# A graph-attention layer on one core: the last 512 columns summed as dense blocks, the last picks and weighings in a new order

## The chip, the cores and the metric

The kernel runs on one core of a Trainium2 chip. The time is device microseconds of one execution; the number for a kernel is the median of its runs. In the profile's terms PE is TensorE, DVE is VectorE, ACT is ScalarE, POOL is GpSimd, SP is the engine that issues most DMAs, and PEld is PE's loading of weights.

## What is computed

`x` is 4096 x 128, `adj` 4096 x 4096 of zeros and ones, sparse (about two ones in a row on average, many more in the first rows and columns). Two layers, each added to `x` behind a layer norm and a ReLU:

```python
h = relu(layernorm(x))
Wh = h @ W
e = leaky_relu((Wh @ a[:128])[:, None] + (Wh @ a[128:])[None, :], 0.2)
mask = (adj > 0) | eye(4096)
x = x + softmax(where(mask, e, -9e15), axis=1) @ Wh

h = relu(layernorm(x))
sens = exp(-(1 / adj - 1) ** 2 / (2 * 0.25))
x = x + where(adj < 1.0, sens, 0.0) @ (h @ W1 + B1)
```

With entries of zero and one the second layer adds nothing (a one is not below the cutoff, and a zero gives exp of minus infinity). The kernel checks every entry for that on DVE and ACT, together with bounds on how many edges it can hold, and has a general path behind a flag for other inputs. With the inputs drawn here the general path isn't run.

## The kernel before

**Tiles and stages.** The 4096 rows are four quarters of 1024 rows. `adj` (64 MB, with its diagonal set to zero on the host) comes in 32 chunks of 2 MB: for each quarter its four blocks of 1024 columns, each in two halves of 512 rows. SP issues them in order into a ring of six slots; a slot is free when the chunk in it has been packed on PE and checked.

**From ones to edges.** PE packs eight rows of a column into one word of bits (`pack`, line 618, with a code of the column from line 614). DVE scans the words with MAX8 over segments of a bank (`scan`, 1139), each step being one block of columns. Then DVE picks the nonzero words of several steps, a piece, out of the candidates (`pick`, 1152 to 1172); PE places them across partitions (`place`, 674 and 681); DVE turns words into row numbers (`decode`, `index` at 1276). What doesn't fit a lane's own slots is shared among the lanes of a set (`pick_shared` 1188 to 1216, `place_shared` 694, `decode_shared`, `shared_index` at 1245). There are five pieces; piece 3 is the steps 12 to 14 and piece 4 is step 15 alone, which hold quarter 3.

**From edges to sums.** POOL fetches for each slot 128 rows of `node_table` (Wh and its scores, in HBM) by an indirect DMA (a gather, line 535), 66 KB each. The slots form groups of eight gathers (four in groups 5 and 9): groups 0 and 1, 3 and 4, 6, and 8 are the own slots of pieces 0, 1, 2 and 3, and groups 2, 5, 7 and 9 the shared slots of pieces 0, 1, 2 and 4. DVE weighs a group: weights from the gathered scores (1315, 1318), spread over 128 columns (1326, 1332 or 1339 by the kind of group). PE scatters the gathered rows with them into the accumulators of the quarter (`scatter`, 744). For the last group this goes by turns of one gather each (`weigh_last` 1354 and 1365, `scatter_last`).

**Beside it.** The first 128 columns, which are dense, are transposed and weighed as a whole (1409, `add_columns` 729). A node's own weight goes by a diagonal (ACT 962, `add_own` 736). A quarter ends with `epilogue` (1420, 1425) and the store of its rows; the last quarter with `finish_last` and `finish` (1435, 1439). `check` is one pass of DVE over a chunk (1111) or two of ACT (929, 938).

**What sets the order.** Each engine's program is written out by hand. It loops over chunks i, and tables say in which iteration a step stands: on DVE `SCAN_AT`, `PICK_AT`, `DECODE_AT`, `EPILOGUE_AT`, `WEIGH_AT`, and `CHECK_LATE` for checks that are put off; on PE `PLACE_AT`, `PLACE_BEHIND`, `SCATTER_AT`, `ADD_COLUMNS_AT`, `ADD_OWN_AT`; on ACT `OWN_WEIGHTS_AT`. What stands behind the loop is written in order. POOL's gathers are in the order of the groups, each waiting for its index and for a free place among the gathered rows. Engines run in order, so an instruction that waits holds all behind it.

## Time and profile before

| | |
|---|---|
| median of 3 runs | 215.99 us (215.91 to 216.35) |
| the profiled execution | 216.57 us, span 214.8 us |
| PE, DVE, ACT, POOL busy | 72%, 83%, 88%, 60% of the span |
| mean granted clock of PE | 0.923 |
| chunk DMAs | 32 of 2 MB; 76.83 MB moved in all, 358 GB/s over the span |

Until about 190 us the DMA engines are busy all the time with the chunks, and the other engines keep up with them at various distances. The last chunk lands at about 191.8 us; what follows is the rest of quarter 3: picking, gathering, weighing, summing and storing. No engine is busy all through that stretch. The busy shares of the whole span therefore say little on it, and the views to read are the chain of waits of the last 75 us and the engines' instructions in order of time in it. Times in these views count from the span's start.

### The profile page before, as it was taken

What the parts mean: (1) busy time and instruction counts of PE and PEld (TensorE: products, weight loads), DVE (VectorE), ACT (ScalarE), POOL (GpSimd) and SP (SyncE); (2) the same over time, 40 slices, a digit from 0 to 9 for tenths busy, and PEclk for the clock granted to TensorE, in tenths of its full rate; (3) what the DMA queues carried; (4) which work ended last, traced back from release to release, by engine and by line L of the source; (5) the groups of instructions that cost most, each with busy time, mean ns of one, the idle gap of its engine ahead of it and who ended that gap; (6) DMA issues with size and microseconds to landing.
All of it is one profiled execution on the core that took longest, in us unless ns stands there. A gap on an engine that the chain in (4) does not pass through costs nothing.

```text
span 214.8 us, 3127 instructions
## 1 busy us (share of the span) xinstructions
PE 155.6 (72%) x914; PEld 102.5 (48%) x928; DVE 177.4 (83%) x529; ACT 189.5 (88%) x207; POOL 129.7 (60%) x140
## 2 busy tenths in 40 slices
PE   0188779994849665599749978599393967799572
PEld 0076565441425342387535635286231654667561
DVE  7993999999997999989474695995796599859855
ACT  0699988499999999999999999799999994999960
POOL 3980002196001788889777888889077788868350
PEclk9999999998888999889976999889878899999887
DMA  5999999999999999999999999999999999972313
GB/s 158 347 415 410 412 406 413 404 410 405 414 421 408 404 392 400 402 393 396 398 388 387 392 403 389 399 389 395 400 408 390 390 397 393 407 283 45 117 23 104
DMA packets 22403, 76.83 MB, mean 358 GB/s; under 512 B 2671, under 2 KB 3270, under 8 KB 22384
## 3 DMA queue, kind: packets, MB, share of 16 engines
q1 hardware_dynamic: 18912, 71.31, 84.9%
q0 software_dynamic: 2912, 5.22, 7.2%
q8 instruction: 8, 0.13, 0.3%
q10 hardware_dynamic: 560, 0.08, 0.2%
q14 instruction: 11, 0.09, 0.1%
HBM read 74.08 MB, written 4.23 MB: 365 GB/s over the span
## 4 chain that ended last, share of the span: by engine, by line
DMA 27%; DVE 27%; PE 19%; issue 11%; POOL 9%; ACT 5%; POOLq 0%; DVEq 0%; ACTq 0%; SPq 0%
DMA adj_ring<-adj_apart 23%; POOL gathered_rows L535 9%; DVE summed L1111 8%; PE bank L618 7%; DMA gathered_rows<-node_table,shared_index 4%; ACT spread L898 3%; PE bank L744 3%; PE bank L653 2%; DVE hub_w L1382 2%; PE bank L729 2%; DVE x_sb L1425 2%; PE bank L736 2%; DVE shared_slots L1197 1%; DVE cand L1139 1%; DVE stats L1091 1%
## 5 line engine op out<-in xcount | busy, mean ns | idle before, releaser
L535 POOL DMA_INDIRECT gathered_rows<-node_table,index x48 | 69.3, 1444 | 38.6 <-DVE index L1276 24.5
L929 ACT ACTIVATE trash_a<-adj_ring,below_one 128x4096 fp8e4<-128x4096 f32 x19 | 70.4, 3704 | 5.3 <-DMA adj_ring<-adj_apart 4.7
L618 PE MATMUL bank<-adj_ring,pack_w 128*128 128x512 bf16 x242 | 70.7, 423 | 4.5 <-DMA adj_ring<-adj_apart 3.4
L938 ACT ACTIVATE trash_a<-adj_ring 128x4096 fp8e4<-128x4096 f32 x19 | 68.7, 3614 | 0.5
L1111 DVE SCALAR_TENSOR_TENSOR summed<-adj_ring 128x4096 fp8e4<-128x4096 f32 x13 | 58.2, 4480 | 7.5 <-DMA adj_ring<-adj_apart 7.4
L535 POOL DMA_INDIRECT gathered_rows<-node_table,shared_index x24 | 36.8, 1535 | 9.8 <-issue 7.0
L618 PEld LDWEIGHTS bank<-adj_ring,pack_w 128*128 128x128 bf16 x248 | 25.0, 103 | 35.5 <-issue 9.8
L1139 DVE MAX8 cand<-bank 128x8 f32<-128x120 f32 (+25 forms) x82 | 23.3, 351 | 2.8 <-PE bank L618 2.8
L744 PE MATMUL bank<-gathered_rows,spread 128*128 128x129 f32 x160 | 21.0, 283 | 3.0 <-DVE spread L1365 1.8
L744 PEld LDWEIGHTS bank<-gathered_rows,spread 128*128 128x128 f32 x160 | 19.5, 196 | 4.8 <-issue 4.4
L614 PE MATMUL bank<-codes,code_w 128*128 128x512 bf16 x24 | 10.6, 443 | 8.7 <-DMA adj_ring<-adj_apart 8.7
L653 PE MATMUL bank<-whe,hub_w 128*128 128x129 f32 x64 | 10.2, 316 | 5.7 <-DVE hub_w L1386 5.7
L898 ACT ACTIVATE spread<-x_sb,shift,rstd 128x128 f32<-128x128 f32 x32 | 13.3, 501 | 0.3 <-DVE shift L1103 0.3
L653 PEld LDWEIGHTS bank<-whe,hub_w 128*128 128x128 f32 x64 | 9.4, 225 | 7.2 <-DVE hub_w L1386 6.9
L482 POOL PARTITION_ALL_REDUCE ends_all<-ends x1 | 1.4, 1440 | 17.4 <-DVE ends L1507 17.4
L556 PE MATMUL bank<-ident,spread 128*128 128x128 f32 x32 | 6.5, 337 | 7.2 <-ACT spread L898 7.2
L568 PE MATMUL bank<-w_sb,gathered_rows 128*128 128x130 f32 x64 | 10.6, 318 | 1.2 <-ACT whe L912 0.9
L568 PEld LDWEIGHTS bank<-w_sb,gathered_rows 128*128 128x128 f32 x64 | 9.5, 227 | 2.4 <-ACT gathered_rows L904 1.8
L614 PEld LDWEIGHTS bank<-codes,code_w 128*128 128x128 bf16 x32 | 3.8, 119 | 13.7 <-DMA adj_ring<-adj_apart 10.4
L1409 DVE SCALAR_TENSOR_TENSOR col_w<-r_rows,hub_whe,bank 128x512 f32<-128x512 f32 (+1 forms) x6 | 4.2, 701 | 7.1 <-PE bank L598 7.1
L962 ACT ACTIVATE own_w<-ident,w_self 128x128 f32<-128x128 f32 x32 | 9.7, 386 | 0.2 <-PE bank L736 0.2
L1382 DVE TENSOR_SCALAR hub_w<-r_hub,whe 128x128 f32<-128x128 f32 x32 | 8.9, 352 | 0.0
(188 smaller groups left out, 237.0 us busy)
## 6 DMA issues: line engine op xcount, KB each, us to landing
adj_ring<-adj_apart SPq DMA_DIRECT2D x32, 2048.0 KB, 23.3
node_table<-gathered_rows POOLq DMA_DIRECT2D x4, 520.0 KB, 9.3
x_sb<-in_x SPq DMA_DIRECT2D x8, 256.0 KB, 5.8
out<-x_sb SPq DMA_DIRECT2D x3, 512.0 KB, 14.4
gathered_rows<-node_table,index POOLq DMA_INDIRECT x48, 5.6
gathered_rows<-node_table,shared_index POOLq DMA_INDIRECT x24, 5.7
out<-x_sb SPq DMA_DIRECT2D x2, 192.0 KB, 2.0
out<-x_sb SPq DMA_DIRECT2D x1, 128.0 KB, 2.0
```

What stands on the lines that cost most here:

```text
L535: pool.indirect_dma_start(out=rows[:, g % RING_GROUPS * GE + t, :], out_offset=None, in_=table, in_offset=bass.IndirectOffsetOnAxis(ap=row ...
L568: last = nc.tensor.matmul(bank[6 + half][:, b * (D + 2):(b + 1) * (D + 2)], hT[:, nb * P:(nb + 1) * P], w0_sb[:, :], start=(b == 0), stop= ...
L614: nc.tensor.matmul(to[:, :], code_w[:, 2 * c + half, :], codes[:, :], start=True, stop=False, skip_group_check=True)
L618: last = nc.tensor.matmul(to[:, :], pack_w[:, k, :], ring_hi[:, i % AR, at:at + BW], start=False, stop=(k == KB - 1), skip_group_check=True)
L653: last = nc.tensor.matmul(bank[7][:, 0:E1], hub_w[:, m % 2, b, :], whe[:, 4 * HUB_ORDER[m] + b, ONE:ONE + E1], start=(m + b == 0), stop=(m ...
L744: return nc.tensor.matmul(acc_of(SUPER_OF_GROUP[g], t), spread[:, g % 2, at * KB:(at + 1) * KB, :], rows[:, g % RING_GROUPS * GE + turn, G ...
L898: last = nc.scalar.activation(hn_block(b), x_sb[:, b, :], ACT.Identity, bias=shift[:, b:b + 1], scale=rstd[:, b:b + 1])
L929: nc.scalar.activation(trash_a[:, :], ring[:, i % AR, :], ACT.Sign, bias=below_one[:, :], scale=-1.0, accum_out=signs[:, n:n + 1], saturat ...
L938: nc.scalar.activation(trash_a[:, :], ring[:, i % AR, :], ACT.Abs, accum_out=sizes[:, n:n + 1], saturate=False).then_inc(checked_a, 1)
L1111: nc.vector.scalar_tensor_tensor(trash_v, ring[:, i % AR, :], 1.0, ring[:, i % AR, :], ALU.is_ge, ALU.not_equal, accum_out=bad_v[:, n:n + ...
L1139: last = nc.vector.max(cand[:, at * 8:(at + 1) * 8], word_bank(step, half)[:, lo:hi])
L1382: last = nc.vector.tensor_scalar(hub_w[:, m % 2, b, :], r_hub[:, :], whe[:, nb, QA:QA + 1], whe[:, nb, AA:AA + 1], ALU.mult, ALU.max)
```

## The change

For quarter 3 the chunks are cut in another way. Chunk 28 is 512 columns (2048 to 2559) of all 1024 rows; chunks 29 and 30 are columns 1024 to 2047 in two halves; chunk 31 is the last 512 columns (2560 to 3071), laid out by the host with columns on partitions: four blocks of 128 columns x 1024 rows, each with a DMA and a semaphore of its own. Chunk 31 is neither packed nor scanned. DVE makes a block's weights in one instruction (`weigh_dense`), and PE adds the block with eight matmuls (`add_dense`). The rows of `node_table` for these 512 columns (`dense_whe`) come by one DMA on SP ahead of chunk 20 and lie in `summed`; checks from chunk 14 on therefore write their unused result to `hub_mask`, and the dense weights lie in the ring slot of chunk 26.

Piece 2's shared slots go to sets of eight lanes instead of four, so that group 7 has four gathers instead of eight. Two tables of factors (`r_oct2`, halves of `r_quad`) change with it.

The order: pick(3) in iteration 29 rather than 30, and PE's place(3) directly behind pack(29); weigh(7), which stood behind the loop, in iteration 28; check(26) in iteration 26 behind weigh(5), rather than 27; epilogue(1) at 27 and epilogue(2) at 30; scatters, column sums and own sums accordingly; ACT's own weights of quarter 3 at 29.

```diff
+NARROW, DENSE = 28, CHUNKS - 1
 def chunk(i):
+    if i >= NARROW:
+        return SG - 1, 1 if i in (29, 30) else 2, int(i > 29)
...
-PIECES = [..., ((8, 9, 10, 11), 24, 8, 32, 4),
+PIECES = [..., ((8, 9, 10, 11), 24, 8, 32, 8),
...
-CHECK_LATE = {22: 22, 27: 26, 29: 28}
-SCAN_AT = {2 * n + 2: n for n in range(STEPS - 1)}
-PICK_AT = {8: 0, 16: 1, 24: 2, 30: 3}
-DECODE_AT = {9: 0, 17: 1, 25: 2, 31: 3}
+CHECK_LATE = {22: 22, 26: 26, 28: 28}
+SCAN_AT = {**{2 * n + 2: n for n in range(STEPS - 2)}, 29: 14}
+PICK_AT = {8: 0, 16: 1, 24: 2, 29: 3}
+DECODE_AT = {9: 0, 17: 1, 25: 2, 30: 3}
...
-WEIGH_AT = {13: 0, 17: 1, 18: 2, 21: 3, 25: 4, 26: 5, 28: 6}
-SCATTER_AT = {14: 0, 17: 1, 19: 2, 22: 3, 26: 4, 27: 5, 30: 6}
-PLACE_AT = {8: 0}
-PLACE_BEHIND = {15: 1, 23: 2, 29: 3}
+WEIGH_AT = {13: 0, 17: 1, 18: 2, 21: 3, 25: 4, 26: 5, 27: 6, 28: 7}
+SCATTER_AT = {14: 0, 17: 1, 19: 2, 22: 3, 25: 4, 26: 5, 28: 6, 29: 7}
+PLACE_AT = {8: 0, 29: 3}
+PLACE_BEHIND = {15: 1, 23: 2}
...
-ADD_COLUMNS_AT = {13: 0, 21: 1, 28: 2}
-EPILOGUE_AT = {20: 0, 28: 1}
-OWN_WEIGHTS_AT = {8: 0, 17: 1, 22: 2, CHUNKS: 3}
-ADD_OWN_AT = {13: 0, 21: 1, 29: 2}
+ADD_COLUMNS_AT = {13: 0, 21: 1, 27: 2}
+EPILOGUE_AT = {20: 0, 27: 1, 30: 2}
+OWN_WEIGHTS_AT = {8: 0, 17: 1, 22: 2, 29: 3}
+ADD_OWN_AT = {13: 0, 21: 1, 27: 2}
...
+                if i == DENSE:
+                    for b in range(DB):
+                        sp.dma_start(dense_adj[:, b, :], adj_tail[1, b]).then_inc(dense_ready[b], 16)
+                    return
...
+                if i == 20:
+                    sp.wait_ge(table_stored, 16 * SG)
+                    sp.wait_ge(checked_v, DVE_CHECKED.index(14))
+                    sp.dma_start(dense_whe, table[DENSE_AT:DENSE_AT + BW, :].rearrange("(p b) c -> p b c", b=DB)).then_inc(
+                        dense_whe_loaded, 16)
...
+            def add_dense(b):
+                pe.wait_ge(dense_set, b + 1)
+                pe.wait_ge(dense_whe_loaded, 16)
+                for t in range(KB):
+                    nc.tensor.matmul(acc_of(SG - 1, t), dense_w[:, b, t, :], dense_whe[:, b, GQ:GQ + E1], start=False,
+                                     stop=True, skip_group_check=True)
...
-            scatter(7)
+            add_columns(SG - 1, range(6))
+            add_own(SG - 1, range(6))
             place(4)
-            add_columns(SG - 1)
+            add_columns(SG - 1, range(6, KB))
+            add_own(SG - 1, range(6, KB))
+            add_dense(0)
             place_shared(4)
-            add_own(SG - 1)
+            add_dense(1)
+            add_dense(2)
             scatter(8)
+            add_dense(3)
             scatter_last(0)
...
+            def weigh_dense(b):
+                dve.wait_ge(dense_ready[b], 16)
+                if b == 0:
+                    dve.wait_ge(dense_whe_loaded, 16)
+                    dve.wait_ge(packed, 27)
+                    dve.wait_ge(col_turned, 2 * (SG - 1) + 1)
+                    dve.wait_ge(checked_v, DVE_CHECKED.index(26) + 1)
+                nc.vector.scalar_tensor_tensor(dense_w[:, b, :, :].rearrange("p t m -> p (t m)"),
+                                               r_rows[:, :, :].rearrange("p t m -> p (t m)"), dense_whe[:, b, AQ:AQ + 1],
+                                               dense_adj[:, b, :], ALU.max, ALU.mult).then_inc(dense_set, 1)
...
-            weigh(7)
             scan(STEPS - 1)
             pick(4)
-            epilogue(2)
+            weigh_dense(0)
             pick_shared(4)
+            weigh_dense(1)
             decode_shared(4)
+            weigh_dense(2)
             weigh(8)
+            weigh_dense(3)
             weigh_last(0)
```

What the tables do to the engines' order stands out at three places. The first is DVE behind weigh(5), whose last row is the spread at 1339 (now 1439). In the kernel before, with 1409 the column products (`col_w`) of chunks 26 and 27, 1111 the check of chunk 26 and 1139 scan(13):

```order
L1339 TENSOR_TENSOR spread<-same,hq_of_e 128x512 x2
L1409 SCALAR_TENSOR_TENSOR col_w<-r_rows,hub_whe,bank 128x8x64
L1111 SCALAR_TENSOR_TENSOR summed,bad<-adj_ring 128x4096
L1409 SCALAR_TENSOR_TENSOR col_w<-r_rows,hub_whe,bank 128x8x64
L1139 MAX cand<-bank 128x8 x5
```

And now, where 1180 is the check and 1509 the first column product:

```order
L1406 TENSOR_TENSOR same<-r_pair,gathered_rows 128x128
L1409 TENSOR_TENSOR same<-same,shared_on 128x128
L1439 TENSOR_TENSOR spread<-same,hq_of_e 128x512 x2
L1180 SCALAR_TENSOR_TENSOR hub_mask,bad<-adj_ring 128x4096
L1509 SCALAR_TENSOR_TENSOR col_w<-r_rows,hub_whe,bank 128x8x64
```

The check of chunk 26 has gone ahead of the first column product. The second place is DVE from there to the check of chunk 28. In the kernel before (1139 scan(13), then weigh(6) to 1326, epilogue(1) to 1425, the check, scan(14) and the start of pick(3)):

```order
L1139 MAX cand<-bank 128x8 x5
L1315 TENSOR_TENSOR edge_w<-r_slots,gathered_rows 128x64
L1318 TENSOR_TENSOR edge_w<-edge_w,bits_i 128x64
L1326 TENSOR_TENSOR spread<-edge_w,lane_of_p 128x1024
L1420 RECIPROCAL rden<-bank 128x3 x2
L1420 RECIPROCAL rden<-bank 128x2
L1425 SCALAR_TENSOR_TENSOR x_sb<-bank,rden,x_sb 128x128 x8
L1111 SCALAR_TENSOR_TENSOR summed,bad<-adj_ring 128x4096
L1139 MAX cand<-bank 128x8 x5
L1152 TENSOR_REDUCE fullest<-cand 128x1
```

And now (1520 and 1525 epilogue(1), 1406 to 1417 weigh(6), 1509 the second column product, 1208 scan(13), 1406 with `r_oct` to 1430 weigh(7), 1180 the check):

```order
L1520 RECIPROCAL rden<-bank 128x3 x2
L1520 RECIPROCAL rden<-bank 128x2
L1525 SCALAR_TENSOR_TENSOR x_sb<-bank,rden,x_sb 128x128 x8
L1406 TENSOR_TENSOR edge_w<-r_slots,gathered_rows 128x64
L1409 TENSOR_TENSOR edge_w<-edge_w,bits_i 128x64
L1417 TENSOR_TENSOR spread<-edge_w,lane_of_p 128x1024
L1509 SCALAR_TENSOR_TENSOR col_w<-r_rows,hub_whe,bank 128x8x64
L1208 MAX cand<-bank 128x8 x5
L1406 TENSOR_TENSOR same<-r_oct,gathered_rows 128x256
L1409 TENSOR_TENSOR same<-same,shared_on 128x256
L1430 TENSOR_TENSOR spread<-same,quad_of_e 128x512 x2
L1180 SCALAR_TENSOR_TENSOR hub_mask,bad<-adj_ring 128x4096
```

epilogue(1) has gone ahead of weigh(6), and weigh(7), which stood behind pick_shared(3), ahead of the check of chunk 28. The third place is PE's tail. In the kernel before, from the packing of chunk 30 on (618; 744 is a scatter, 674 place(4), 729 the columns, 694 place_shared(4), 736 the own sums):

```order
L618 MATMUL bank<-adj_ring,pack_w 128x512 x4
L744 MATMUL bank<-gathered_rows,spread 128x129 x8
L618 MATMUL bank<-adj_ring,pack_w 128x512 x8
L744 MATMUL bank<-gathered_rows,spread 128x129 x8
L674 MATMUL bank<-slots,own_oct 16x8 x8
L729 MATMUL bank<-hub_whe,col_w 128x129 x8
L694 MATMUL bank<-turn_of_tq,stats 128x4
L736 MATMUL bank<-whe,own_w 128x129 x8
L744 MATMUL bank<-gathered_rows,spread 128x129 x16
```

And now, from scatter(7) on (806 is a scatter, 676 the packing of chunk 30, 789 the columns, 797 the own sums, 732 place(4), 772 the dense blocks, 752 place_shared(4)):

```order
L806 MATMUL bank<-gathered_rows,spread 128x129 x8
L676 MATMUL bank<-adj_ring,pack_w 128x512 x8
L789 MATMUL bank<-hub_whe,col_w 128x129 x6
L797 MATMUL bank<-whe,own_w 128x129 x6
L732 MATMUL bank<-slots,own_oct 16x8 x8
L789 MATMUL bank<-hub_whe,col_w 128x129 x2
L797 MATMUL bank<-whe,own_w 128x129 x2
L772 MATMUL bank<-summed,adj_ring 128x129 x8
L752 MATMUL bank<-turn_of_tq,stats 128x4
L772 MATMUL bank<-summed,adj_ring 128x129 x16
L806 MATMUL bank<-gathered_rows,spread 128x129 x8
L772 MATMUL bank<-summed,adj_ring 128x129 x8
```

scatter(7) has moved from behind the last packing to ahead of it, where it follows place(3); one block of eight dense matmuls stands ahead of place_shared(4), two behind it, and one between scatter(8) and the last scatters.

## Rows read from the trace of the kernel before

**Rows 1.** Chain of waits, 140 to 215: start us, length us, what it was

```profile
180.07 5.01 POOL gathered_rows L535
...
185.38 6.33 DMA gathered_rows<-node_table,shared_index
...
211.78 0.61 DVE x_sb L1439 x2
```

**Rows 2.** POOL in time: start us, us, line, operation [idle before, what ended it]

```profile
169.26 0.99 POOL L535 DMA_INDIRECT gathered_rows<-node_table,shared_index  x1 [0.30 <-issue]
170.56 4.33 POOL L535 DMA_INDIRECT gathered_rows<-node_table,shared_index  x1 [0.30 <-issue]
...
188.89 1.08 POOL L535 DMA_INDIRECT gathered_rows<-node_table,index  x1 [1.42 <-DVE index L1276]
...
192.90 1.91 POOL L535 DMA_INDIRECT gathered_rows<-node_table,index  x1 [0.30 <-issue]
...
204.12 1.21 POOL L535 DMA_INDIRECT gathered_rows<-node_table,shared_index  x1 [0.30 <-issue]
...
206.94 1.00 POOL L535 DMA_INDIRECT gathered_rows<-node_table,shared_index  x1 [0.30 <-issue]
```

**Rows 3.** DVE in time, 163 to 213, columns as before

```profile
163.44 1.34 DVE L1339 TENSOR_TENSOR spread<-same,hq_of_e 128x512 f32<-128x512 f32 x2
...
169.60 4.42 DVE L1111 SCALAR_TENSOR_TENSOR summed<-adj_ring 128x4096 fp8e4<-128x4096 f32 x1
...
179.79 4.42 DVE L1111 SCALAR_TENSOR_TENSOR summed<-adj_ring 128x4096 fp8e4<-128x4096 f32 x1
...
184.13 1.49 DVE L1139 MAX8 cand<-bank 128x8 f32<-128x24 f32 x5
...
187.95 0.17 DVE L1276 SCALAR_TENSOR_TENSOR index<-words_i,empty_i 128x8 int32<-128x8 int32 x1
...
191.79 0.43 DVE L1315 TENSOR_TENSOR same<-r_quad,gathered_rows 128x256 f32<-128x256 f32 x1 [2.13 <-DMA gathered_rows<-node_table,shared_index]
...
192.72 1.23 DVE L1332 TENSOR_TENSOR spread<-same,quad_of_e 128x1024 f32<-128x1024 f32 x1
193.87 1.43 DVE L1139 MAX8 cand<-bank 128x8 f32<-128x272 f32 x4
...
196.37 2.16 DVE L1425 SCALAR_TENSOR_TENSOR x_sb<-bank,rden,x_sb 128x128 f32<-128x128 f32 x8
...
201.87 0.16 DVE L1245 TENSOR_TENSOR shared_index<-shared_column,shared_empty 128x4 int32<-128x4 int32 x1
...
202.73 0.22 DVE L1315 TENSOR_TENSOR edge_w<-r_slots,gathered_rows 128x64 f32<-128x64 f32 x1
...
203.24 1.22 DVE L1326 TENSOR_TENSOR spread<-edge_w,lane_of_p 128x1024 f32<-128x1024 f32 x1
...
208.88 0.17 DVE L1435 RECIPROCAL rden<-bank 128x3 f32<-128x3 f32 x1
```

**Rows 4.** DMA issues, 160 to 190: bytes each, median us to landing

```profile
gathered_rows<-node_table,shared_index POOLq DMA_INDIRECT x8, 5.9
```

**Rows 5.** DMA issues, 188 to 210

```profile
gathered_rows<-node_table,index POOLq DMA_INDIRECT x8, 3.2
```

**Rows 6.** PE in time, 160 to 213, columns as in rows 2

```profile
164.55 0.39 PE L614 MATMUL bank<-codes,code_w 128*128 128x512 bf16 x1 [3.46 <-DMA adj_ring<-adj_apart]
164.77 1.87 PE L618 MATMUL bank<-adj_ring,pack_w 128*128 128x512 bf16 x4
...
176.42 1.06 PE L618 MATMUL bank<-adj_ring,pack_w 128*128 128x512 bf16 x4
...
194.09 2.02 PE L744 MATMUL bank<-gathered_rows,spread 128*128 128x129 f32 x16 [0.26 <-DVE spread L1332]
```

**Rows 7.** ACT in time, 175 to 213, columns as in rows 2

```profile
181.44 3.71 ACT L929 ACTIVATE trash_a<-adj_ring,below_one 128x4096 fp8e4<-128x4096 f32 x1 [2.83 <-DMA adj_ring<-adj_apart]
```

**Rows 8.** Stretch: engines' busy us (count), then PEclk, DMA share, GB/s

```profile
164.50:168.50 4.00, 3.95 (x12) 1.46 (x13) 0.28 (x1) 3.97 (x3) 3.09 (x4) 0.57 1.03 389
```

More of the change, by code:

```diff
@@ L61, in chunk, with banks_of, step_of, packed_by @@
     return s, (first + i % (2 * CC) // 2) % CC, i % 2
+def banks_of(step):
+    c = chunk(2 * step)[1]
+    return [2 * c] if 2 * step == NARROW else [2 * c, 2 * c + 1]
+def step_of(i):
+    return STEPS - 1 if i in (29, 30) else i // 2
+def packed_by(step):
+    return 2 * step + 2 if step < STEPS - 2 else 2 * step + 1
+def scanned_by(step):
+    return sum(len(banks_of(m)) for m in range(step + 1))
 def column_step(s):
     return next(n for n in range(CC * s, CC * s + CC) if chunk(2 * n)[1] == 0)
-PIECES = [((0, 1, 2, 3), 32, 16, 32, 4), ((4, 5, 6, 7), 24, 16, 16, 4), ((8, 9, 10, 11), 24, 8, 32, 4),
+PIECES = [((0, 1, 2, 3), 32, 16, 32, 4), ((4, 5, 6, 7), 24, 16, 16, 4), ((8, 9, 10, 11), 24, 8, 32, 8),
           ((12, 13, 14), 16, 8, 0, 8), ((15,), 8, 0, 32, 8)]
@@ L101, in piece_segments @@
     s = SUPER_OF_PIECE[n]
-    columns = {chunk(2 * step)[1] for step in PIECES[n][0]}
-    return [x for x in SEGMENTS[s] if x[0] // 2 in columns]
+    banks = {b for step in PIECES[n][0] for b in banks_of(step)}
+    return [x for x in SEGMENTS[s] if x[0] in banks]
 NCAND = max(len(piece_segments(n)) for n in range(len(PIECES))) * 8
@@ L292, in gnn_program @@
         oct_words = placed[0:LANES, 1, :]
[L293 removed]
+        s_by_oct = [general_mem[:, NB * 32 + n * KB * KB * OL:NB * 32 + (n + 1) * KB * KB * OL] for n in range(2)]
         verdict = cand[:, 0:NBAD]
@@ L792, in _ @@
             lane_scores()
-            for i in range(CHUNKS):
+            for i in range(DENSE):
                 pack(i)
```

190 lines of the change are left out of this document (120 added, 70 removed).

## The prediction

> **What bounds the kernel now.** I read the chain of waits first, for the last 75 us, then the orders in time of the engines that it names. Up to 160 us the chain is mostly the stream of adjacency chunks; from there to the end it is POOL and DVE by turns. Two of POOL's gathers, which take 1.00 us elsewhere, stand there with 5.01 and 4.33 us; then comes the landing of the rows that the last of group 7's gathers fetched, 6.33 us from 185.38 [rows 1, 2]. weigh(7) waits 2.13 us for those rows [rows 3]. The chain goes on over scan(15), epilogue(2), pick_shared(4) and the last four gathers, and ends with the output tiles of quarter 3.
>
> The long gathers have one cause that the trace repeats. Gather 170.56 starts under check(26) (169.60 + 4.42 = 174.02) and ends at 174.89; gather 180.07 starts under check(28) (to 184.21) and ends at 185.08; gather 192.90 starts under the spread of weigh(7) (to 193.95) and ends at 194.81 [rows 1 to 3]. So a gather that begins while DVE runs an instruction with two operands in SBUF ends 0.87 us after that instruction. Undisturbed, gathers follow one another every 1.30 us [rows 2].
>
> **Part 1, the last 512 columns are summed densely.** Removed: packing and scanning of these columns, before a half of chunks 30 and 31. Added on DVE: four products of 128x1024. None is in the trace; a quarter of a check (4.42 for 4096 elements) is 1.10, and the spread of 128x1024 takes 1.23 [rows 3]. I take 1.2: 4.8 us in four pieces. Added on PE: four times eight matmuls of the 128x129 form; eight (16 passes in the trace) take 2.02 [rows 6], so 8.1 us, of which three blocks lie in PE's waits before group 8 is weighed. The fourth does not: it stands between scatter(8) and the last scatters, +2.0. The dense rows' table (0.27 MB more on SP) is as much as the four gathers of 66 KB that group 7 loses, so the chunks should keep their times. ACT's own_weights(3) goes into the 2.83 us for which ACT waits for chunk 29 [rows 7]: no gain and no loss, because ACT is not in the chain there.
>
> **Part 2, check(26) goes behind weigh(5).** weigh(5) ends at 163.44 + 1.34 = 164.78, and chunk 26 is there at 164.55 [rows 3, 6]. The check starts between 164.9 and 165.9; I take 165.4, so it ends at 169.8. It now catches another gather: the eighth of group 6, at 169.26 - 2 x 1.30 = 166.66, ends at 170.7 (0.87 behind) rather than 167.7. Group 7 has four gathers instead of eight; they start at 171.0, 172.3, 173.6 and 174.9. Under this load a gather lands 5.9 us after its start [rows 4], so the group's rows are there at 180.8; with 0.3 either way I take 180.5. Before, they were there at 191.7.
>
> **Part 3, weigh(7) goes ahead of check(28) and of the third pick.** DVE gets to it at about 179: group 6's held gather lands 4.9 behind its end, at 175.6; weigh(6) 1.7 like weigh(8), scan(13) at most scan(14)'s 1.49, and the column product, half of a dense one, 0.6 [rows 3]. Then it waits for group 7 until 180.5, in place of the 2.13 us before. Behind that waiting instruction on DVE stand check(28), scan(14) and pick(3), and for these wait place(3) on PE, and then POOL, which has nothing to fetch until index(3). weigh(7) took 2.16 (191.79 to 193.95); with its spread in two halves 2.3: to 182.8. check(28) takes 4.34 up to scan(14) (179.79 to 184.13): 187.1. scan(14) has two segments instead of five, 1.49 x 2/5 = 0.6, I take 0.7: 187.8. From the end of the scan (185.62) to index(3) it is 2.33 [rows 3]: index(3) at **190.1, against 187.95**. That is +2.15, the step on which the forecast rests most. epilogue(2) is no longer between pick(4) and pick_shared(4), but ahead of scan(15), which is worth 2.4 to DVE's tail; the products take more than that back.
>
> **Part 4, twelve gathers in a row.** The first gather starts 0.94 after index(3) [rows 2, 3]: 191.04. Eight of group 8 and four of the last group follow: 191.04 + 12 x 1.30 - 0.30 = 206.3 if nothing holds them. Before, the last ended at 206.94 + 1.00 = 207.94 [rows 2]. But the dense products and the spread of weigh(8) now lie over just these gathers. Each can hold one back by 0 to 1.0 us (spread 192.72 cost 0.91, spread 203.24 cost 0.21) [rows 2, 3], five of them by 0 to 5; I take 0.55 each, the mean of the two, of which 1.9 falls on group 8 in front of its eighth gather (three products and a part of a fourth instruction). That gather ends at 191.04 + 8 x 1.30 - 0.30 + 1.9 = 203.0, so counts from 202.0; it lands 3.2 later [rows 5], at 205.2. weigh(8) takes 1.73 (202.73 to 204.46) [rows 3]: 206.9. Before: 204.46, so +2.4.
>
> DVE itself is ready by then: epilogue(2) ends near 194.3 (2.4 of work behind scatter(7), which PE reaches after place(3)), scan(15) takes 1.43, with pick(4) 2.0, so with the first product 197.5; pick_shared(4) and the index took 3.34 behind epilogue(2) (198.53 to 201.87), with the second product in between 202.0; the third 203.7 [rows 3]. So group 8's rows are what comes last, by 1.5.
>
> **The end.** PE: scatter(8) 206.9 to 208.8, the fourth dense block to 210.7, two short scatters to 211.5. From the start of finish_last(0), which follows them, to the last output tile it was 208.88 to 212.39 [rows 1, 3], 3.5: to 215.0, **+2.6**.
>
> **PE's clock.** Where PE had waited 3.46 us for chunk 26, four packing matmuls behind took 1.87 against 1.06 elsewhere, and the granted clock of that stretch was 0.57, near the lower of the two levels (1.2 of 2.4 GHz) [rows 6, 8]. In the new order PE has nothing between pack(29), done near 184.6, and place(3) near 188.7, a wait of 4 us, so scatter(7) and pack(30) can run at half: 0 to +1.5 on epilogue(2) and scan(15), most of it hidden behind the gathers. I take +0.4.
>
> Sum: +3.0. The profiled execution took 216.57 us with a span of 214.8; it would be 219.6, and the median of the runs is 0.58 lower: **219.0**.
>
> **A rule of the skill against it.** The trace shows gathers held by DVE, but not the reverse: check(26) at 169.60 began under gather 169.26 (to 170.25) and took 4.42, the same as check(28) at 179.79, under which none was running when it began [rows 1 to 3]. The Trainium skill (SBUF — State Buffer, "SBUF: two separate sides") says of the port pair that the two engines share that whichever starts first gets it for the whole instruction and the other is fully blocked. By that rule a product would wait for the gather under it as well, which is rival D. The row speaks against it, for this form of instruction.
>
> **The rivals.**
> A. As forecast, +3.0.
> B. About as before. The products slip past the gathers' starts (0.6 instead of 1.9 on group 8), PE stays at its upper level (-0.4) and group 7's rows land at 179.5 (-1.0): -2.7, so 216.3. For it: spread 203.24 cost only 0.21.
> C. Faster. These products, and check(26) where it now stands, do not hold gathers as the three instructions of the trace did. Group 7's rows are then there before DVE is (179), so index(3) comes 1.5 sooner; group 8 loses its 1.9, the clock's 0.4 goes, and the last two PE blocks run 0.3 closer: 219.0 - 4.1 = 214.9. It decides in favour of the change when the sum of holds on groups 6 to 8 is under about 1 us. Against it: all three long gathers follow the same rule to 0.02 us.
> D. Worse. The products wait for gathers as well as holding them: five by half of a gather's 1.00 is +2.5, 221.5.
> E. The change doesn't do what it says: a word with more edges than its slots now hold sends the kernel down its general path, many times the time. Counted from the reference's inputs, the fullest words fit; 0.01.
>
> **How the numbers follow.** A 0.58, B 0.20, C 0.16, D 0.05, E 0.01. A spreads from 217 to 221.5 with the holds (0 to 5) and the landing (179 to 181.5). The range leaves out half of C and half of D, and E: 215.0 to 221.5. A measurement of this kernel tells 0.2% (0.43 us) from no change, so "same" is 215.56 to 216.42. Of C 0.13 is faster and 0.03 the same; of B 0.03 faster, 0.07 the same, 0.10 slower; A, D and E are slower. Together: faster 0.16, same 0.10, slower 0.74.
>
> **What would show it.** Right: DVE waits at weigh(7) until 180 to 181; index(3) at 189.5 to 190.7, its first gather 0.94 later; the eighth gather of group 6 with 3 to 4.4 us; twelve gathers without a wait for an index between them, some of 1.3 to 2.0; weigh(8) ending at 206 to 208. Wrong: no wait at weigh(7), or index(3) before 188.5; a wait of POOL for shared_index (then the products on DVE, not the gathers, set the end); a granted clock of 1 behind place(3) takes the 0.4 off; and if DVE is still at weigh_last when the last dense block ends, the 2.0 for that block is wrong.

## The result and the profile after

| | before | changed |
|---|---|---|
| median | 216.17 us (215.91 to 216.86, 4 runs) | 220.38 us (220.02 to 220.50, 4 runs) |
| profiled execution, span | 216.57, 214.8 | 220.36, 218.6 |
| ratio of the runs | | 1.0177 (95%: 1.0148 to 1.0205) |
| index(3) starts at | 187.95 | 190.95 |
| from there to the last output tile | 24.44 | 25.33 |
| last output tile done | 212.39 | 216.28 |

By the ratio of the runs the change costs 1.5 to 2.0%, about 3.8 us; the two medians lie 4.2 us apart. The profiled executions differ by 3.89 us in the end of the last output tile: 3.00 of it is there when index(3) starts, 0.89 comes behind it.

The page of the changed kernel: the span, the busy times, the granted clock in 40 slices, and two lines on the chain that ended last.

```profile
span 218.6 us, 3283 instructions
PE 161.4 (74%) x993; PEld 108.3 (50%) x993; DVE 182.0 (83%) x533; ACT 190.1 (87%) x209; POOL 121.1 (55%) x136
PEclk9999999997967998899958999999579999769999
## 4 chain that ended last, share of the span: by engine, by line
DMA 32%; DVE 28%; PE 23%; issue 9%; ACT 5%; SPq 2%; DVEq 0%; ACTq 0%
```

POOL, which had 9% of the chain before, is out of it, and PE has gone from 19% to 23%. The four gathers saved show in POOL's busy time (129.7 to 121.1 us). The granted clock has a dip to 7 and 6 tenths in slices 35 and 36 (186 to 197 us), where it had its full value before (1.00 from 182 to 202). The kernel before has a dip of its own, 0.57 from 202 to 206.

DVE in order of time in the changed kernel, to compare with [rows 3] (lines moved: 1180 is a check, 1350 index(3), 1369 a dense product, 1319 shared_index, 1406 and 1439 belong to the weighings, 1454 to weigh_last, 1520 is epilogue(2), 1535 finish_last):

```profile
164.93 1.34 DVE L1439 TENSOR_TENSOR spread<-same,hq_of_e 128x512 f32<-128x512 f32 x2
166.19 4.41 DVE L1180 SCALAR_TENSOR_TENSOR hub_mask<-adj_ring 128x4096 fp8e4<-128x4096 f32 x1
...
175.92 0.23 DVE L1406 TENSOR_TENSOR edge_w<-r_slots,gathered_rows 128x64 f32<-128x64 f32 x1 [2.37 <-issue]
...
181.23 0.42 DVE L1406 TENSOR_TENSOR same<-r_oct,gathered_rows 128x256 f32<-128x256 f32 x1 [1.65 <-issue]
...
183.36 4.42 DVE L1180 SCALAR_TENSOR_TENSOR hub_mask<-adj_ring 128x4096 fp8e4<-128x4096 f32 x1
...
190.95 0.17 DVE L1350 SCALAR_TENSOR_TENSOR index<-words_i,empty_i 128x8 int32<-128x8 int32 x1
...
194.32 0.30 DVE L1520 RECIPROCAL rden<-bank 128x3 f32<-128x3 f32 x3 [1.66 <-PE bank L806]
...
198.63 1.28 DVE L1369 SCALAR_TENSOR_TENSOR adj_ring<-r_rows,summed,adj_ring 128x1024 f32<-128x1024 f32 x1
...
202.39 1.26 DVE L1369 SCALAR_TENSOR_TENSOR adj_ring<-r_rows,summed,adj_ring 128x1024 f32<-128x1024 f32 x1
...
203.96 0.16 DVE L1319 TENSOR_TENSOR shared_index<-shared_column,shared_empty 128x4 int32<-128x4 int32 x1
...
204.82 1.33 DVE L1369 SCALAR_TENSOR_TENSOR adj_ring<-r_rows,summed,adj_ring 128x1024 f32<-128x1024 f32 x1
206.07 0.21 DVE L1406 TENSOR_TENSOR edge_w<-r_slots,gathered_rows 128x64 f32<-128x64 f32 x1
...
211.40 0.28 DVE L1454 SCALAR_TENSOR_TENSOR same<-r_oct,gathered_rows,shared_on 128x64 f32<-128x64 f32 x1 [0.91 <-DMA gathered_rows<-node_table,shared_index]
...
212.76 0.18 DVE L1535 RECIPROCAL rden<-bank 128x3 f32<-128x3 f32 x1 [0.55 <-PE bank L806]
```

Up to index(3) this is what the prediction's parts 2 and 3 describe, about a microsecond later: the check of chunk 26 stands right behind weigh(5), DVE waits 1.65 us in front of weigh(7), and check(28), scan(14) and pick(3) follow. Behind index(3) it is not: DVE waits 1.66 us for scatter(7) in front of epilogue(2), and from there to weigh(8) at 206.07 it works almost without a gap. POOL in the same stretch, against [rows 2]:

```profile
166.85 4.63 POOL L579 DMA_INDIRECT gathered_rows<-node_table,index  x1 [0.30 <-issue]
...
175.69 1.00 POOL L579 DMA_INDIRECT gathered_rows<-node_table,shared_index  x1 [0.30 <-issue]
...
191.90 1.08 POOL L579 DMA_INDIRECT gathered_rows<-node_table,index  x1 [11.16 <-DVE index L1350]
...
198.52 1.00 POOL L579 DMA_INDIRECT gathered_rows<-node_table,index  x1 [0.30 <-issue]
...
201.13 1.00 POOL L579 DMA_INDIRECT gathered_rows<-node_table,index  x1 [0.30 <-issue]
204.89 1.00 POOL L579 DMA_INDIRECT gathered_rows<-node_table,shared_index  x1 [2.77 <-DVE shared_index L1319]
...
207.49 1.18 POOL L579 DMA_INDIRECT gathered_rows<-node_table,shared_index  x1 [0.30 <-issue]
```

The eighth gather of group 6 is held as forecast (4.63 us, 0.88 behind the check's end at 170.60), and group 7's last gather lands 5.5 us after 175.69. But group 8's eight gathers run through unheld: the first dense product starts 0.11 us after the sixth gather (198.63 and 198.52) and ends 0.08 us into the seventh, and the second comes when all eight are done. POOL then waits 2.77 us for shared_index, as it did before the change (2.79 us), so the twelve are not in a row. PE in order of time, and three stretches of it (columns as in rows 8):

```profile
189.54 0.57 PE L732 MATMUL bank<-slots,own_oct 128*16 128x8 f32 x16 [4.36 <-issue]
...
190.49 3.79 PE L806 MATMUL bank<-gathered_rows,spread 128*128 128x129 f32 x16
194.07 2.37 PE L676 MATMUL bank<-adj_ring,pack_w 128*128 128x512 bf16 x8
...
209.88 1.95 PE L772 MATMUL bank<-summed,adj_ring 128*128 128x129 f32 x16
```

```profile
185.20:189.50 4.30, 0.00 (x0) 0.00 (x0) 4.16 (x10) 4.27 (x4) 0.00 (x0) 0.83 1.02 412
189.50:194.00 4.50, 4.46 (x34) 4.47 (x35) 2.16 (x13) 4.47 (x4) 1.80 (x2) 0.50 0.58 231
194.00:198.00 4.00, 4.00 (x26) 2.69 (x25) 3.68 (x16) 3.97 (x4) 3.08 (x4) 0.89 0.19 47
```

PE does nothing for 4.36 us ahead of place(3), and scatter(7) then runs at 0.50 of the full clock, the lower of the two levels (1.2 of 2.4 GHz): 3.79 us against 2.02 in [rows 6]. That is the wait in front of epilogue(2).

### The profile page after: what moved, and what is told of

It reads as the page before. It is cut to its first block, busy times and chain, and to the rows that moved or that the text cites. A ratio compares the mean times of both kernels' runs of the same rounds, so it can differ in the third digit from the quotient of the medians.

```text
span 218.6 us, 3283 instructions
## 1 busy us (share of the span) xinstructions
PE 161.4 (74%) x993; PEld 108.3 (50%) x993; DVE 182.0 (83%) x533; ACT 190.1 (87%) x209; POOL 121.1 (55%) x136
## 4 chain that ended last, share of the span: by engine, by line
DMA 32%; DVE 28%; PE 23%; issue 9%; ACT 5%; SPq 2%; DVEq 0%; ACTq 0%
DMA adj_ring<-adj_apart 32%; DVE summed L1180 8%; PE bank L676 8%; PE bank L806 5%; ACT spread L963 3%; DVE hub_w L1482 3%; DVE cand L1208 3%; PE bank L772 2%; PE bank L672 2%; PE bank L789 2%; DVE x_sb L1525 2%; PE bank L797 2%; SPq L438 2%; DVE adj_ring L1369 1%; DVE stats L1158 1%
## 5 line engine op out<-in xcount | busy, mean ns | idle before, releaser
L579 POOL DMA_INDIRECT gathered_rows<-node_table,index x48 | 73.2, 1525 | 47.9 <-DVE index L1350 34.2
L676 PE MATMUL bank<-adj_ring,pack_w 128*128 128x512 bf16 x232 | 66.5, 420 | 4.6 <-DMA adj_ring<-adj_apart 4.6
L676 PEld LDWEIGHTS bank<-adj_ring,pack_w 128*128 128x128 bf16 x232 | 23.6, 104 | 35.9 <-issue 9.9
L1180 DVE SCALAR_TENSOR_TENSOR hub_mask<-adj_ring 128x4096 fp8e4<-128x4096 f32 x6 | 26.5, 4417 | 6.9 <-DMA adj_ring<-adj_apart 6.9
L1180 DVE SCALAR_TENSOR_TENSOR summed<-adj_ring 128x4096 fp8e4<-128x4096 f32 x7 | 31.4, 4492 | 0.1
L579 POOL DMA_INDIRECT gathered_rows<-node_table,shared_index x20 | 23.9, 1193 | 8.6 <-issue 5.5
L806 PEld LDWEIGHTS bank<-gathered_rows,spread 128*128 128x128 f32 x160 | 20.6, 206 | 3.0 <-issue 2.5
L672 PE MATMUL bank<-codes,code_w 128*128 128x512 bf16 x30 | 13.5, 451 | 5.4 <-DMA adj_ring<-adj_apart 5.4
L711 PEld LDWEIGHTS bank<-whe,hub_w 128*128 128x128 f32 x64 | 8.2, 200 | 8.8 <-DVE hub_w L1486 8.6
L772 PE MATMUL bank<-summed,adj_ring 128*128 128x129 f32 x64 | 8.0, 278 | 1.3 <-DVE adj_ring L1369 1.3
```

Source lines behind the costliest of these rows:

```text
L579: pool.indirect_dma_start(out=rows[:, g % RING_GROUPS * GE + t, :], out_offset=None, in_=table, in_offset=bass.IndirectOffsetOnAxis(ap=row ...
L672: nc.tensor.matmul(to[:, :], code_w[:, 2 * c + half, :], codes[:, :], start=True, stop=False, skip_group_check=True)
L676: last = nc.tensor.matmul(to[:, :], pack_w[:, k, :], ring_hi[:, i % AR, at:at + BW], start=False, stop=(k == KB - 1), skip_group_check=True)
L711: last = nc.tensor.matmul(bank[7][:, 0:E1], hub_w[:, m % 2, b, :], whe[:, 4 * HUB_ORDER[m] + b, ONE:ONE + E1], start=(m + b == 0), stop=(m ...
L806: return nc.tensor.matmul(acc_of(SUPER_OF_GROUP[g], t), spread[:, g % 2, at * KB:(at + 1) * KB, :], rows[:, g % RING_GROUPS * GE + turn, G ...
L1180: nc.vector.scalar_tensor_tensor(trash_v[int(i >= 14)], ring[:, i % AR, :], 1.0, ring[:, i % AR, :], ALU.is_ge, ALU.not_equal, accum_out=b ...
```

## Experiments

Four things could stand behind the 3.9 us: the load of the dense rows' table, weigh(7) ahead of the third pick, PE's clock, and the dense work itself. Here is what each kernel gave; the ratio is to the kernel before on the same chip, and the last three columns, in us, are from the profiled execution.

| kernel | ratio (95%) | index(3) | from there to the last tile | last tile |
|---|---|---|---|---|
| before | 1 | 187.95 | 24.44 | 212.39 |
| changed | 1.0177 (1.0148 to 1.0205) | 190.95 | 25.33 | 216.28 |
| e1 table loaded late | 1.0170 (1.0132 to 1.0208) | 190.07 | 25.33 | 215.40 |
| e2 weigh(7) behind the pick | 1.0141 (1.0110 to 1.0173) | 187.07 | 29.82 | 216.89 |
| e3 PE kept busy | 1.0134 (1.0094 to 1.0174) | 190.78 | 24.96 | 215.74 |
| e4 nothing dense | 1.0093 (1.0057 to 1.0129) | 191.34 | 23.56 | 214.90 |
| e5 e2 with PE kept busy | 1.0119 (1.0068 to 1.0169) | 186.62 | 28.34 | 214.96 |
| e6 nothing dense, PE kept busy | 1.0045 (1.0020 to 1.0069) | 189.43 | 23.77 | 213.20 |
| e7 e1, e5, epilogue(2) later | 0.9987 (0.9957 to 1.0017) | 186.53 | 26.30 | 212.83 |
| e8 e7, shared index first | 1.0188 (1.0153 to 1.0224) | 186.11 | 30.92 | 217.03 |
| e9 e7, two steps reordered | 0.9958 (0.9935 to 0.9981) | 186.02 | 25.42 | 211.44 |
| e10 eight lanes alone | 1.0008 (0.9979 to 1.0038) | 188.49 | 24.43 | 212.92 |

The profiled execution is one of the timed ones. It lies between 0.4 us under and 1.4 us over its kernel's median, and index(3) shifts with the stream of chunks: e4 changes nothing ahead of index(3) and has it 0.4 us later than the changed kernel, e6 has the same work there as e3 and has it 1.35 us earlier. A difference of less than a microsecond in these columns therefore proves little by itself.

**e1: the table's load.**

```diff
-                if i == 20:
+                if i == DENSE:
                     sp.wait_ge(table_stored, 16 * SG)
```

> The load of the dense rows' table goes from ahead of chunk 20 to ahead of chunk 31. Theory: that load sets the chunk stream back (chunk 26 landed at 166.08 against 164.50), and check(26), the held eighth gather, group 7's rows, weigh(7), check(28) and index(3) hang on chunk 26; chunks 20 to 30 land 0.9 to 1.2 us earlier and the time falls by as much, to 219.2 to 219.5. Rival: the stream is late for another reason or has slack here; the time stays within 0.4 us of the changed kernel's 220.38.

The first packing of chunk 20 in the kernel before, the changed one and e1:

```profile
131.40 0.39 PE L614 MATMUL bank<-codes,code_w 128*128 128x512 bf16 x1 [0.41 <-DMA adj_ring<-adj_apart]
```

```profile
132.36 0.39 PE L672 MATMUL bank<-codes,code_w 128*128 128x512 bf16 x1 [0.89 <-DMA adj_ring<-adj_apart]
```

```profile
131.71 0.39 PE L672 MATMUL bank<-codes,code_w 128*128 128x512 bf16 x1 [0.41 <-DMA adj_ring<-adj_apart]
```

The stream of chunks as a whole lies up to a microsecond earlier or later from one execution to the next, so one pair of times says little here. The gap between two landings says more: in the six profiled executions with the load ahead of chunk 20 (changed, e2 to e6) that chunk landed 6.25 to 6.48 us behind chunk 19, in five without it (before, e1, e7, e8, e10; e9's landing is not in its trace) 5.56 to 5.58. So the load costs the stream 0.7 to 0.9 us at this place, and most of it stays: from the landing of chunk 16 to that of chunk 30 it is 79.5 to 80.1 us in the six and 79.0 to 79.4 in the five. In e1 index(3) and the last tile are both 0.88 us earlier. The timed runs put e1 at 219.76 us, 0.6 below the changed kernel but within the intervals of both ratios: the mechanism is shown at chunk 20, its worth in the whole time is not told from zero.

**e2: weigh(7) behind the pick.**

```diff
-WEIGH_AT = {..., 27: 6, 28: 7}
-SCATTER_AT = {..., 28: 6, 29: 7}
+WEIGH_AT = {..., 27: 6}
+SCATTER_AT = {..., 28: 6, 30: 7}
...
                     pick_shared(DECODE_AT[i])
+                    if DECODE_AT[i] == HANDED:
+                        weigh(7)
```

> weigh(7) goes behind the third pick's pick_shared(3), where it was before, and scatter(7) behind the packing of chunk 30; all else as changed. Theory (weigh(7)'s wait of 1.65 and its 2.13 us of work stand in front of index(3)): index(3) at 187.2 instead of 190.95, PE's wait ahead of place(3) shrinks from 4.36 to about 1 us and its granted clock stays at the upper level; weigh(7) then ends at 191.0, scatter(7) at 193.0, epilogue(2) starts at 193.0 instead of 194.32: 1.3 us less, 219.1. Rival (index(3) hangs on the chunks or on the pack of chunk 28, not on weigh(7)): index(3) after 189.5, and the time 220.4 to 222.5, since weigh(7)'s 2.1 us now stand behind it.

DVE (first two lines) and PE in e2:

```profile
187.07 0.17 DVE L1350 SCALAR_TENSOR_TENSOR index<-words_i,empty_i 128x8 int32<-128x8 int32 x1
...
194.92 0.30 DVE L1520 RECIPROCAL rden<-bank 128x3 f32<-128x3 f32 x3 [3.96 <-PE bank L806]
```

```profile
187.76 2.76 PE L676 MATMUL bank<-adj_ring,pack_w 128*128 128x512 bf16 x8 [0.99 <-DMA adj_ring<-adj_apart]
191.11 3.78 PE L806 MATMUL bank<-gathered_rows,spread 128*128 128x129 f32 x16 [0.59 <-DVE spread L1430]
```

index(3) is where the theory put it, 3.9 us sooner. But in the profiled execution PE, with waits of 0.6 to 1.2 us, falls to 0.57 of its clock from 187.7 on all the same, scatter(7) takes 3.78 us, and DVE waits 3.96 us for it; the last tile comes no sooner. This execution, with 221.08 us, is the slowest of e2's five. The other four took 219.23 to 219.74, some 0.6 to 1.2 us under the changed kernel's median and not far from the theory's 219.1. Three of them have a mean granted clock of 0.94 over the span against 0.91 in the profiled one; whether the clock stayed up behind index(3) in these, no trace shows. The ratio is not apart from the changed kernel's by the intervals. So the theory's step on the path is right, its step on the clock failed in the execution that can be read, and what weigh(7)'s place is worth by itself stays open.

**e3: PE kept busy.**

```diff
+                if i == 29:
+                    pe.wait_ge(scanned, scanned_by(12))
+                    for k in range(18):
+                        nc.tensor.matmul(bank[1][:, :], pack_w[:, k % KB, :], codes[:, :], start=True, stop=True,
+                                         skip_group_check=True)
                 if i in PLACE_AT:
```

> 18 matmuls into an unused bank are put on PE between the packing of chunk 29 and place(3), with no other change; their result is not used. Theory: PE's clock fell to its lower level behind the 4.36 us in which it had nothing to do, and scatter(7) with 3.79 us kept DVE waiting 1.66 us in front of epilogue(2); with the clock kept up scatter(7) takes 2.0, the wait is 0 to 0.2 and the end comes 1.5 to 1.7 us earlier, 218.8. Rival (as predicted, most of the slow clock is hidden behind the gathers): 0.4 or less, 220.0 or more.

PE, DVE and POOL in e3 (1374 is a dense product, 1411 weigh(8)):

```profile
190.32 2.03 PE L806 MATMUL bank<-gathered_rows,spread 128*128 128x129 f32 x16
```

```profile
196.75 1.28 DVE L1374 SCALAR_TENSOR_TENSOR adj_ring<-r_rows,summed,adj_ring 128x1024 f32<-128x1024 f32 x1
...
200.50 1.26 DVE L1374 SCALAR_TENSOR_TENSOR adj_ring<-r_rows,summed,adj_ring 128x1024 f32<-128x1024 f32 x1
...
205.53 0.28 DVE L1411 TENSOR_TENSOR edge_w<-r_slots,gathered_rows 128x64 f32<-128x64 f32 x1 [1.26 <-issue]
```

```profile
197.03 1.87 POOL L579 DMA_INDIRECT gathered_rows<-node_table,index  x1 [0.30 <-issue]
...
200.50 2.14 POOL L579 DMA_INDIRECT gathered_rows<-node_table,index  x1 [0.31 <-issue]
```

scatter(7) is back at 2.03, epilogue(2) starts at 192.42 without a wait, 1.9 us sooner. Only 0.54 of this reaches the last tile (0.96 in the medians, 219.42 against 220.38). The dense products, now earlier, lie over the gathers of group 8 and hold two of them (1.87 and 2.14 us, ending 0.87 and 0.88 behind the product), and weigh(8) waits 1.26 us. The profile names nothing that ended this wait, but the last of group 8's gathers landed at 205.45, just ahead of it. This is the mechanism of the prediction's part 4. The clock alone does not decide whether it comes: with the clock kept up as well, e5 has no gather of group 8 held, and e7 and e9 have one each.

**e4 and e6: nothing dense**, without and with e3's matmuls. Every `weigh_dense` and `add_dense` is taken out, so these kernels leave out 512 columns of quarter 3.

> The four dense products on DVE and the four dense blocks on PE are left out, so the last quarter's sums lack 512 columns; loads, checks and all else stay. Theory (DVE's own work sets the tail): weigh(8) starts 3.6 us earlier at 202.4, the last four gathers from 202.5, the end about as in the kernel before, 4.0 to 4.4 us earlier, 216.2. Rival (as predicted, group 8's gathers set weigh(8), and only the last PE block is on the path): no gather had been held by a product, so 2.0 us earlier, 218.4.

> As e4 (dense products and blocks left out, so 512 columns lack in the last quarter's sums), with e3's 18 unused matmuls ahead of place(3). Theory (three limits close together: DVE's dense work, PE's clock, the held gathers; in e4 the slow clock took the first one's place): weigh(8) at about 201.0 to 202.0, the last gather ends at about 207.0, the end 3.4 us before e4's and 4.8 before the changed kernel's, 215.6. Rival (the dense work is worth the 2 us of e4 and the clock 0.6 to 0.9 by itself): 217.5 to 218.0.

The rivals' numbers hold in both, 218.42 and 217.70 us, and the theories fall: without the dense work the tail is far from 4 us shorter. The reason that e4's rival gave does not hold: group 8's rows are there at 204.01, and DVE comes to weigh(8) at 205.04 without a wait. In e4 DVE is rid of the 3.6 us of the products and then waits for PE, which packs chunk 30 at half clock (2.88 us), and for place(4) and place_shared(4) (1.12 and 0.60 us). In e6 PE has nothing to do from 199 to 204 once the dense blocks are gone, and pays at the very end: the granted clock is 0.50 from 204 to 210, and DVE waits 2.43 us for PE ahead of finish_last(0). So the clock is not out of the picture there as the theory had it. PE in e6 in that stretch:

```profile
198.66 0.38 PE L752 MATMUL bank<-turn_of_tq,stats 16*128 16x4 f32 x2 [1.59 <-DVE stats L1286]
204.15 6.21 PE L806 MATMUL bank<-gathered_rows,spread 128*128 128x129 f32 x28 [5.11 <-DVE spread L1418]
```

From index(3) to the last tile the dense work is worth 1.2 us with PE kept busy (24.96 in e3, 23.77 in e6) and 1.8 without (25.33, 23.56), of the 4.8 us that DVE spends on it. The ratios make it 1.8 to 1.9 us in both pairs.

**e5: e2 with PE kept busy.**

```diff
+                if i == 29:
+                    keep_up(5)
                 pack(i)
+                if i == 30:
+                    keep_up(6)
...
                     place(PLACE_AT[i])
+                if i == 29:
+                    keep_up(8)
```

Here `keep_up(n)` issues n of e3's matmuls, and e2's edit is in it too.

> As e2 (weigh(7) behind pick_shared(3), scatter(7) behind the packing of chunk 30), and PE kept busy by 19 unused matmuls into a free bank: 5 ahead of pack(29), 8 behind place(3), 6 behind pack(30). Theory (in e2 the 3.7 us earlier index(3) was lost to PE's lower clock, scatter(7) 3.78 us and DVE's wait of 3.96): packing and scatter(7) at 2.0 us each, epilogue(2) starts at 193.1 against 194.92 in e2 and 194.32 in the changed kernel, and the time is 1.2 us under the changed kernel's, 219.2. Rival (weigh(7) behind the pick costs on DVE what it gives on POOL, whatever the clock): 220.0 or more.

epilogue(2) starts at 192.98 and the time is 219.27, as the theory said; the last tile comes at 214.96, 1.32 before the changed kernel's. Of 4.3 us that index(3) gains, 3.0 are given back behind it, since weigh(7) and the wait for scatter(7) (2.47 us) now stand there on DVE. The ratio is not apart from e2's or the changed kernel's by the intervals, so what the unused matmuls bring in e5 is not shown by the timed runs.

**e7: e1 and e5 together, and epilogue(2) behind pick(4).** The last edit:

```diff
-EPILOGUE_AT = {20: 0, 27: 1, 30: 2}
+EPILOGUE_AT = {20: 0, 27: 1}
...
             pick(4)
+            epilogue(2)
             weigh_dense(0)
```

> e1 and e5 together (table load ahead of chunk 31, weigh(7) behind pick_shared(3), PE kept busy), and epilogue(2) behind pick(4), where it was before the change. Theory (the causes found add up: stream 0.9, weigh(7) ahead of index(3) 3.7, clock 1.9, less what DVE's own work takes back): index(3) at 186.2, weigh(7) ends at 190.1, weigh(8) at 203.7, the end 4.0 to 4.4 us before the changed kernel's, 216.0 to 216.4, level with the kernel before. Rival (the dense products hold gathers as soon as these run under them, up to 1 us each): 217 to 218.

216.39 us, level with the kernel before. DVE's two remaining waits in e7:

```profile
192.89 0.31 DVE L1532 RECIPROCAL rden<-bank 128x3 f32<-128x3 f32 x3 [0.51 <-PE bank L806]
...
209.31 0.18 DVE L1547 RECIPROCAL rden<-bank 128x3 f32<-128x3 f32 x1 [1.55 <-PE bank L806]
```

scan(15) and pick(4) now fill the time in which scatter(7) runs. From e5 to e7 the ratio falls by more than the intervals, and from index(3) to the last tile the profiled execution gains 2.04 us. The late table leaves that stretch as it was in e1 (25.33), so this gain is epilogue(2)'s place. So the 3.8 us that the changed kernel loses can be won back without touching the dense layout, by the order of the steps, the place of the table's load and the 19 unused matmuls together. The same without the matmuls was not run, so it is not shown that the order alone would do.

**e8: the shared index ahead of the products.**

```diff
-            weigh_dense(0)
             pick_shared(4)
-            weigh_dense(1)
             decode_shared(4)
+            weigh_dense(0)
+            weigh_dense(1)
             weigh_dense(2)
```

On PE place_shared(4) goes ahead of `add_dense(0)`.

> As e7, with the first three dense products behind decode_shared(4) instead of around it, and place_shared(4) ahead of the dense blocks on PE. Theory (in e7 DVE and PE set the end, the last four gathers come in time): shared_index of piece 4 at 198 instead of 200.1, weigh(8) as in e7, the end the same to 0.4 us earlier, 215.6 to 216.2. Rival (the last gathers set the end in e7): 2.0 us earlier, 214.2.

220.74 us, worse than either said. PE in e8, and a stretch of it:

```profile
198.26 0.38 PE L752 MATMUL bank<-turn_of_tq,stats 16*128 16x4 f32 x2 [1.57 <-DVE stats L1297]
201.32 7.68 PE L772 MATMUL bank<-summed,adj_ring 128*128 128x129 f32 x48 [2.68 <-DVE adj_ring L1381]
```

```profile
198.00:202.00 4.00, 1.05 (x5) 0.97 (x6) 3.56 (x13) 3.97 (x4) 1.68 (x2) 0.60 0.09 20
```

With the products bunched behind the index, PE waits 1.57 and 2.68 us, its clock falls to 0.60 and then 0.55, and three dense blocks take 7.68 us instead of 6.0. scatter(8) starts at 208.84, against 204.64 in e7. Of these 4.2 us 1.7 is the slower clock; the rest is that all three blocks now begin at 201.32, where in e7 the first had run at 196.95. The blocks had also been PE's filling. Neither theory had the clock or this queue on PE in it.

**e9: two steps of e7 reordered.**

```diff
-            epilogue(2)
             weigh_dense(0)
+            epilogue(2)
...
-            finish_last(0)
             weigh_last(3)
+            finish_last(0)
```

> As e7, with the first dense product ahead of epilogue(2) instead of behind it, and weigh_last(3) ahead of finish_last(0). Theory (in e7 DVE works without a gap from 188 to 205 but for 0.51 us in which it waits for scatter(7), and then waits 1.55 us for PE while weigh_last(3) stands behind that wait): the product fills the first wait, -0.5, and weigh_last(3) with 0.8 us the second, -0.8; the end 1.3 us before e7's, 215.1, below the kernel before by 0.6 to 0.8%. Rival (the product holds a gather of group 8, or the last gather lands after the wait): as e7, level with the kernel before.

215.47 us against 216.31 for the kernel before in the same runs: 0.9958 (0.9935 to 0.9981), 1.39 us before e7 in the last tile, 0.88 of it behind index(3). That is less than the theory's 0.6 to 0.8%, but clear of no change: e9 is faster than the changed kernel, and by 0.2 to 0.65% faster than the kernel before. From e7 the intervals do not part it. DVE in e9:

```profile
191.85 1.28 DVE L1381 SCALAR_TENSOR_TENSOR adj_ring<-r_rows,summed,adj_ring 128x1024 f32<-128x1024 f32 x1
193.06 0.30 DVE L1532 RECIPROCAL rden<-bank 128x3 f32<-128x3 f32 x3
```

Both waits are gone. The product did hold a gather of group 8 (1.62 us), as the rival had it, but weigh(8) did not wait for it.

**e10: eight lanes alone.** The kernel before with piece 2's sets of eight lanes, hence four gathers in group 7; the order and the chunks are those of before.

> The kernel before with one part of the change alone: piece 2's shared slots in sets of eight lanes, so that group 7 has four gathers instead of eight; chunks, order and tail as before, nothing dense. Theory (in the kernel before the 2.13 us wait for group 7's rows lay beside another: scan(15) needs the packing of chunk 31, which landed at 191.80 and was packed at 193.83): the wait at weigh(7) is gone, scan(15) still starts at 193.6 to 194.0, and the time is within 0.4 us of the kernel before. Rival (that wait was the path, as the chain of waits has it): 2.1 us less than the kernel before.

DVE in e10 (1371 with `r_oct` is weigh(7), 1173 scan(15)):

```profile
190.16 0.43 DVE L1371 TENSOR_TENSOR same<-r_oct,gathered_rows 128x256 f32<-128x256 f32 x1
...
194.21 1.43 DVE L1173 MAX8 cand<-bank 128x8 f32<-128x272 f32 x4 [1.83 <-PE bank L647]
```

1.0008 (0.9979 to 1.0038): no gain, to within some 0.5 us. The wait for gathered rows that the chain of waits names in the kernel before [rows 1, 3] goes, and a wait of 1.83 us for the packing of chunk 31 comes up one step behind it. It had been there all the time, underneath.

## Why the prediction was right, point by point

- **Direction and size.** +3.0 was forecast, to 219.0; the ratio of the runs gives +3.8, and the median is 220.4, inside the range. Up to index(3) the change came by the mechanism forecast. That the part behind index(3) fits as well, +0.85 forecast (3.0 - 2.15) and +0.89 in the trace, is luck: another wait sets it, as part 4 and the clock below show.
- **The first reading of the chain: too strong.** "Mostly the stream" up to 160 us isn't what the page shows: chunk loads are 23% of the whole chain, about 50 of these 160 us. Nothing in the forecast rests on this.
- **"The chunks should keep their times": wrong.** The table's load goes in ahead of chunk 20, while the four gathers that it was set against are dropped 40 us later. Their bytes are equal, but a queue that is full at 130 us isn't relieved by a gap at 175: e10 drops the same four gathers, loads no table, and its stream from chunk 16 to chunk 30 is no shorter (79.25 us, 79.00 in the kernel before). e1 and the gaps in landing put the load at 0.7 to 0.9 us.
- **Part 2, the held gather: right in kind.** It takes 4.63 us, a little more than the sign named (3 to 4.4). weigh(7) gets group 7's rows at 181.2, 0.7 later than forecast, with the stream.
- **Part 3, weigh(7) ahead of the third pick: right, and the largest term.** +2.15 was forecast for index(3), +3.00 was measured, of which 0.7 to 0.9 is the stream. With weigh(7) behind the pick e2 and e5 have index(3) at 187.07 and 186.62. That it can be avoided at no cost elsewhere was not forecast and isn't so: e5 gains 1.3 at the end, the rest only with epilogue(2)'s place and the late table (e7).
- **Part 4, twelve gathers in a row, held by the products: didn't occur here, and this is the step that failed.** The forecast has group 8's rows come last, at 205.2, 1.5 us after DVE is ready at 203.7. In the trace the two have changed places. The eighth gather starts at 201.13; with the 2.5 us that e3's took from start to landing, its rows are there at about 203.6 (an estimate, since this landing is not in the trace). DVE comes to weigh(8) at 206.07, 2.4 later than forecast: 0.85 of it is index(3), the rest is the wait for scatter(7). Both ways weigh(8) starts 15.1 us behind index(3), which is chance. The sign named beforehand, a wait of POOL for shared_index, is there with 2.77 us, but the kernel before had one of 2.79, so it tells little. The mechanism itself is real: in e3 two gathers are held exactly so.
- **PE's clock: right in kind, too small, and on another path.** 0.4 was taken from a span of 0 to 1.5, "most of it hidden behind the gathers". The trace has 1.66 on DVE's path, since DVE's own work and not the gathers were the limit.
- **epilogue(2) ahead of scan(15): the wrong way round.** The forecast counts this as a gain of 2.4 for DVE's tail. But it is there that DVE waits for scatter(7): 1.66 us in the changed kernel and 2.47 in e5, against 0.51 in e7, where epilogue(2) stands behind pick(4) again.
- **The last dense block: on the path, but worth less than 2.0.** The sign for this was named too, and it is there: DVE is at its third weigh_last at 211.40, held up by gathered rows, when the block is still running (to 211.83). It then waits 0.55 us for PE, so about as much would be gained without the block (an estimate). The forecast's sum is not far off even so: it has 0.2 between weigh(8) and the end (2.4 there, 2.6 at the end), the trace 0.54 (3.34 and 3.88).
- **Rival D.** The four products took 1.26 to 1.33 us, the first from 0.11 us into a gather 1.28, so DVE was not made to wait for a gather's length. By the Trainium skill's rule (SBUF — State Buffer, "SBUF: two separate sides") the engine that comes second is fully blocked in either direction; these runs show that for POOL behind DVE alone.

What stays open: how the whole +3.8 splits among stream, order and clock in timed runs. The single steps e1, e2 and e3 lie within each other's intervals, and e5 is not apart from the changed kernel either; their split rests on profiled executions. Of the variants of the changed kernel that keep all columns only e7 and e9 are apart from it by more than the intervals; e4 and e6, which leave out the dense work, are too. epilogue(2)'s place was not tried in the changed kernel by itself.

## What to carry to other kernels

A wait that the chain of waits names is worth removing only down to the next one beneath it: ask for each wait on the path what the waiting step would need next, and when that is ready (e10: 2.13 us removed, nothing gained). Work that is moved ahead of a pick or an index delays everything that this index starts, on three engines. Putting the wait behind such a step brought index(3) forward by about 4 us here, but most of that was lost at the next wait on DVE until that one was moved as well (e2, e5, then e7). And an order that leaves TensorE idle for some microseconds can pay again afterwards in its clock (4.36 us in the changed kernel, 5.11 in e6): look at the granted clock of the stretch behind every new gap. Unused matmuls in the gap kept it up in e3; work that has to be done anyway does the same, as the dense blocks in e3 (without them, in e6, the clock falls). Last, look at how far the execution that was profiled lies from the median before it is made to speak for all of them (e2).
